# Part border at row tile 42, and the seven row tiles behind it routed as four and three and lined up together

## The reference

```python
xn = _layernorm(x, axis=-1)
x = x + _L0_gnn_ref(xn, src, dst, edge_weight, gnn_weight) + _L0_mix_ref(xn[None], Wqkv, Wout, bout)[0]
x = x + _L0_ffn_ref(_layernorm(x, axis=-1)[None], gate_w, gate_b, w1, b1, w2, b2, gamma, beta)[0]

# _L0_gnn_ref: msgs = x[src] * edge_weight; agg = segment_sum(msgs, dst); agg @ weight      (106250 edges)
# _L0_mix_ref: linear attention, 8 heads of 64; k and v normed per head; out = q (k^T v) / n; Wout, bout
# _L0_ffn_ref: 16 experts, each row goes to its 2 best, weighted by the softmax of the two gate values
h = relu(x @ w1[e] + b1[e])            # 256 -> 512
expert_out = h @ w2[e] + b2[e]         # 512 -> 256
y = x + sum_k topk_w[k] * expert_out[topk_idx[k]]
layernorm(y) * gamma + beta
```

## Time and profile before

| | us |
|---|---|
| median of three runs (1539.89 to 1551.32) | 1547.52 |
| the profiled execution | 1542.19 |
| its span | 1540.5 |
| PE busy | 1077.3 (70%) |
| POOL busy | 1004.7 (65%) |
| DVE busy | 636.2 (41%) |
| ACT busy | 430.5 (28%) |
| mean granted clock of TensorE | 0.867 |

### The profile page before, as it was taken

The page is one execution under the profiler, slowest core; times in us unless marked ns, Lnnn a source line. Parts: engine busy times, 40 slices in busy tenths (PEclk is TensorE's granted clock), DMA queues, the critical chain, the costliest instruction groups (busy, mean ns, idle before and its releaser), DMA issues. The chain is left out here.

```text
span 1540.5 us, 23825 instructions
## 1 busy us (share of the span) xinstructions
PE 1077.3 (70%) x6790; PEld 819.6 (53%) x6790; DVE 636.2 (41%) x2282; ACT 430.5 (28%) x1141; POOL 1004.7 (65%) x1094
## 2 busy tenths in 40 slices
PE   0199989988665979634389659645998975477860
PEld 0055545545543868522278548424876764467750
DVE  7445545543455412324113512250225224554568
ACT  4144434432222333201133223112333322233320
POOL 3477777777647657777767776777776770753425
PEclk9999999999776989965699869866999998599985
DMA  9576566533324888533589479436857770699974
GB/s 337 163 234 221 179 221 194 168 106 104 99 60 149 282 304 299 194 103 105 173 281 343 143 237 344 143 106 228 295 175 220 257 269 14 236 389 317 320 243 136
DMA packets 154922, 323.13 MB, mean 210 GB/s; under 512 B 24768, under 2 KB 97472, under 8 KB 154656
## 3 DMA queue, kind: packets, MB, share of 16 engines
q0 software_dynamic: 49296, 134.68, 27.8%
q1 hardware_dynamic: 65632, 148.16, 27.5%
q10 hardware_dynamic: 39856, 38.67, 7.6%
HBM read 257.06 MB, written 64.36 MB: 209 GB/s over the span
## 5 line engine op out<-in xcount | busy, mean ns | idle before, releaser
L825 POOL DMA_INDIRECT ring<-normed_rows,src_sb x831 | 797.3, 959 | 345.8 <-issue 287.9
L1583 PE MATMUL ps<-room 128*128 128x128 f32 x1888 | 253.5, 292 | 24.6 <-DMA room<-in_w1b 24.2
L1583 PEld LDWEIGHTS ps<-room 128*128 128x128 f32 x1888 | 242.6, 208 | 29.3 <-issue 21.5
L1596 PE MATMUL ps<-room 128*128 128x256 f32 x944 | 227.7, 385 | 11.1 <-issue 10.5
L1451 PE MATMUL ps<-ring,S 128*32 128x256 f32 x1680 | 129.3, 450 | 139.7 <-DMA ring<-normed_rows,src_sb 114.8
L1384 DVE TENSOR_TENSOR desk<-ps,room 128x256 f32<-128x256 f32 x121 | 51.2, 424 | 393.6 <-PE ps L1596 387.3
L1596 PEld LDWEIGHTS ps<-room 128*128 128x128 f32 x944 | 173.2, 194 | 33.4 <-issue 14.2
L1478 PE MATMUL ps<-room,tT 128*128 128x512 f32 x392 | 180.2, 603 | 0.0
L937 ACT ACTIVATE room<-ps,room 128x128 f32<-128x128 f32 x472 | 134.5, 368 | 162.2 <-PE ps L1583 160.5
L816 POOL DMA_INDIRECT ring<-results_by_slot,slot_i x98 | 95.8, 977 | 107.1 <-issue 44.6
L1451 PEld LDWEIGHTS ps<-ring,S 128*32 128x32 f32 x1680 | 57.5, 124 | 188.2 <-issue 158.4
(11 more groups left out here) (206 smaller groups left out, 1255.3 us busy)
## 6 DMA issues: line engine op xcount, KB each, us to landing
room<-in_w2b SPq DMA_DIRECT2D x92, 640.0 KB
room<-in_w1b SPq DMA_DIRECT2D x92, 514.0 KB, 6.4
room<-rows_by_slot SPq DMA_DIRECT2D x121, 128.0 KB
results_by_slot<-desk ACTq DMA_DIRECT2D x121, 128.0 KB
rows_by_slot<-desk ACTq DMA_DIRECT2D x6, 2432.0 KB
ring<-normed_rows,src_sb POOLq DMA_INDIRECT x831
normed_rows<-X SPq DMA_DIRECT2D x7, 896.0 KB, 8.2
result<-ring SPq DMA_DIRECT2D x49, 128.0 KB, 4.6
```

Of the source, the lines that this page charges most:

```text
L825: pool.indirect_dma_start(out=ring[:, b % 2 * BT + m, :], out_offset=None, in_=table, in_offset=bass.IndirectOffsetOnAxis(ap=src_sb[:, b * ...
L1583: mm = pe.matmul(hps[g % 2][:, f * TS:(f + 1) * TS], w1_sb[g % WB][:, k * F + f * P:k * F + (f + 1) * P], xgT[g % 2][:, k, :], start=(k == ...
L1596: mm = pe.matmul(ops, hT[g % 2][:, f, :], w2_sb[g % WB][:, f * D:(f + 1) * D], start=(f == 0), stop=(f == FC - 1))
```

## The change

Four things. The border of the parts moves from row tile 36 to 42, and the subs are cut anew: 24 to 31, 32 to 37, 38 to 41 behind the third, then 42 to 45 and 46 to 48 (before 24 to 29, 30 to 35, 36 to 41, 42 to 46, 47 and 48). The second last sub is JOINED: it gets slots and a scatter but no visits of its own; its full tiles are held, and lined up with those of the last sub, expert by expert, in one run of 25. JOINED was empty before, so the code for it in `line_up`, `runs` and SP's `moe` stood unused. ON_TIME: in slots 68 and 69 the plan adds a visit only if it fits ahead of the landing of the next batch. And a mix that is left for the tail is put first in it.

```diff
-PT = (0, 36, NT)
-SUB = (0, 8, 16, 24, 30, 36, 42, 47, NT)
+PT = (0, 42, NT)
+SUB = (0, 8, 16, 24, 32, 38, 42, 46, NT)
...
-JOINED = ()
+JOINED = (NSUB - 2,)
...
+ON_TIME = 2
+
...
     def chain(work, b):
 
+        if b == NB and mixes:
+
+            g = mixes.pop(0)
+            cost = MIX_PE * (GROUPS[g][1] - GROUPS[g][0])
+            gates.append((g, now + cost + BEHIND[1]))
+            work.append(("mix", g))
+            return cost
...
-        while now < landing(b, b + 1) + LAG:
+        while now < landing(b, b + 1) + (LAG if b < NB - ON_TIME else 0.0):
...
             now += chain(work, b)
-            now += expert(work, b)
+            if b < NB - ON_TIME or now + TAKEN_PE < landing(b, b + 1):
+                now += expert(work, b)
```

## The result

| | before | changed |
|---|---|---|
| median of the runs beside each other | 1547.87 (four) | 1564.47 (four, 1563.02 to 1565.84) |
| ratio, 95% interval | 1 | 1.0109, 1.0077 to 1.0141 |
| the profiled execution, its span | 1542.19, 1540.5 | 1564.56, 1562.8 |
| visits, fresh loads | 118, 92 | 119, 92 |
| T, the end of the last visit | 1492.3 | 1499.8 |

T is here, as in the prediction, the end of PE's last second layer. The changed kernel is slower by 1.1%. Measured once more in another set of runs it had 1569.92 against 1546.84, ratio 1.016 (1.0125 to 1.0195). Both ratios are above 1.01; the interval of the first reaches down to 1.0077. All lines of the changed kernel stand ten higher than before (L1583 is L1593, L1402 is L1412, L825 is L835, L816 is L826).

A forecast was written before the change was run, and what follows sets the result against it. No one engine bounds it all; the end is T plus DVE's finishing work behind it. +4 at T and +15.5 behind it took span 1540.5 to 1560, median said 1565; forecast 1555 to 1577 (chance 0.50), whole range 1537 to 1585.

The forecast's parts named there:

- Total work: Whole kernel: routing rules applied give 119 visits and 92 fresh loads, against 118 and 92 before.
- Start: PE's last long supply of visits, when run 4 begins: at 1127.8 instead of 1060.6, with 63 visits left.
- Slots 60 to 69: PE's stretch before the tail, never without a visit: slot by slot 181.3 us, so the tail begins at 1309.
- rival C: Slower still: POOL's stall comes through, or DVE's slots and line hold tail visits, 10 to 15 more: 1578; chance 0.15.
- The tail of run 5: Slot 70: nine real visits, mix, gates, rank and 8.5 of hold by DVE, 58 us; PE done at 1367.
- The passage: From the end of the tail of run 5 through the left-out run to the joined run's first visit: 14 us, at 1381.
- The joined run: Last run of 25 visits, 16 fresh: 15 x 5.0 + 9 x 3.8 = 109 us, last L1583 at 1490.
- T: End of the last visit: 1490 + 6.3 = 1496.5, that is +4 against the kernel before.
- Behind T: DVE's finishing groups after the last visit: 13 x 4.38 + 2.8, 63.7 us to the end against 48.2, +15.5.
- Sum: Whole kernel: 1540.5 + 4 + 15.5 = 1560 of span; on the median 1567, given as 1565.
- A: Weights no longer late: joined run at 3.8 a step, 91 us, T 18 earlier, 1549; chance 0.22.
- B: Faster: PE packs closer, gates and passages covered, 43 us less, T 1454, 1524; decided by T under 1462; chance 0.13.

The follow-up runs named there:

- Run 4: No follow-up: a run of visits inside the kernel, whose start gives PE its last long supply; first visit at 1060.6 before, 1129.5 in the changed kernel.
- run 8: No follow-up: a run of visits inside the kernel before, 100.6 us for 21 steps, 17 of them into a fresh visit and 4 not.
- packed groups: Both halves of a finishing group between two visits: on the changed kernel 1558.29, ratio 1.0078 (slower chip 2040.66, 1.0063); on the kernel before 2050.05, ratio 1.0094, slower chip.

## Why the prediction was right, point by point

**Total work.** 119 visits and 92 loads, as worked out from the routing rules; L1593 has x1904, 16 to a visit.

**Start.** Said 1127.8, was 1129.5. Run 4's late start is real, and the kernel with an earlier one shows that PE then runs dry instead.

**Slots 60 to 69.** Said 181.3, were 178.0 (1129.47 to 1307.49). The single terms missed by more than their sum: slot 60 took 23.7 for 28, slot 61 17.1 for 19, slot 62 16.4 for 13.5, slot 63 41.0 for 38. The others were within 2. Batch 69 was at 1293.50, said 1294.5. The stop of POOL was 18.9, said 15; batch 66's last gather was issued by 1245 and PE came to it at 1254.5, so it stayed hidden, and that part of rival C is out.

**The tail of run 5.** Said 58 to 1367, was 65 to 1372.9: the worst term, 7 us. The held layer is the row at 1355.33 above. DVE's row of the result before it shows that I named the right cause for it, since it stands directly behind the last operation of the slots:

```profile
1354.67 0.16 DVE L1289 TENSOR_TENSOR prob<-prob 128x3 f32<-128x3 f32 x1
1354.81 0.42 DVE L1394 TENSOR_TENSOR desk<-ps,room 128x256 f32<-128x256 f32 x1
```

But its size was wrong: PE stood idle there for 3.12 us, and I had put 8.5. So all the rest of the tail, which I had at 49.5, took 62.3, and the error in the sum looks smaller than it is. PE waited 3.70 and 2.39 us for ACT and 1.86 for the rank, and ran the tail at a granted clock of 0.84, against 0.94 ahead of it; a first layer took 3.75 us at 1361.07 and 1.95 at 1366.68, which are the two levels, 1.2 and 2.4 GHz. I had priced these visits at 3.9, from a stretch in which the clock stayed up. That the tail came out 7 us dearer is the piece of rival C that came true, but not for C's reason, the hold by DVE, which was smaller than I had put it.

**The passage.** Said 14, was 14.3 (1372.9 to 1387.22).

**The joined run.** Said 109, was 106.4, and 102.8 in the other set. The size was right, the reason only in part. PE's own pace makes 90 of it. Of the 17 us above that, 8.6 are waits for w1 and 2.6 for rows; the first two first layers ran at the lower level of the clock (3.62 and 3.60 us, for 1.95). I took the mean step of run 8, where 21 steps took 22 us above PE's pace and the waits for w1 sum to 13.3, and carried it over to all 15 fresh steps, of which only five waited for w1. With the finishing work largely taken out 98.7 us remain.

**T.** Said 1496.5, was 1499.8. That this is within 3.3 is in part luck: slots 60 to 69 came out 3.3 shorter and the joined run 2.6 shorter than said, start and tail 1.7 and 7 longer.

**Behind T.** Said 63.7, was 63.0: this term carries the verdict. That of the kernel before I explained by DVE's groups "held up a little by picks". The runs with the old border show that the 26 picks give the same 48 us with seven groups, and DVE's waits for picks in the kernel before sum to 2.8 us. The step gave the right number for the changed kernel, where 14 picks need 33 us by estimate and DVE 60. One count in it was short: I had 30 picks left for POOL, and 36 came behind T, the last at 1547.2. That still left DVE's row of the last group, at 1557.8, free of a wait; with packed groups it would be the next limit to look at.

**Sum.** Said 1560 of span, was 1562.8 and 1562.7; 1565 on the median, was 1564.5 and 1569.9. On the spans of the two kernels +7.5 at T and +14.8 behind it make +22.3; the forecast had +4 and +15.5. On the medians it is +16.6 and +23.1.

**The rivals.** A (weights no longer late, T 18 earlier) fell: even with DVE's groups, the stores and most of the picks taken out, T is only 5 us earlier. My argument against it was weaker than it looked. I held 400 GB/s against the best stretch, 331, but the page of the kernel before has a slice of 38.5 us at 389:

```profile
GB/s 337 163 234 221 179 221 194 168 106 104 99 60 149 282 304 299 194 103 105 173 281 343 143 237 344 143 106 228 295 175 220 257 269 14 236 389 317 320 243 136
```

In the window 1348.0 to 1386.4 of that kernel the DMA engines are at a share of 1.02, so 389 is the most that they are seen to move when full, and A's 400 lies above it. What kept A from coming true are the 17 us above PE's pace, told under the joined run. Weights were still late where the DMA engines were near full, and not where they weren't. Two windows of the changed kernel; the first has no wait for w1, the second has two, 2.09 and 1.56 us:

```profile
1440.00:1460.00 20.00, 19.11 (x132) 17.60 (x132) 12.58 (x38) 8.22 (x28) 11.35 (x12) 1.00 0.78 243
1460.00:1480.00 20.00, 15.72 (x104) 13.92 (x104) 10.31 (x32) 6.42 (x22) 7.59 (x8) 1.00 0.96 312
```

A mean over the run, 302 GB/s, hides this. The Trainium skill, "DMA: Bandwidth & Descriptors", section Bandwidth, on which A leaned, puts a ceiling of 435 GB/s beside one of about 358 for what a core moves from and to HBM; the slice of 389 lies between the two: it is above the second, and no run here reaches the first. B (T under 1462) fell by 38 us: gates waited as before, and the passage was paid in full. C is true in part, as told: the tail was 7 us dearer, with a hold by DVE of 3 us in it; POOL's stop did not come through.

## What to carry to other kernels

A border behind which results may be used only all together sets two things at once: how late the finishing work can begin, and how much of it must come last. Before moving one to fill a hole ahead of it, count the finishing groups that will stand behind the last visit and price them at the full time of their engine; here that term of 15 us was paid, and the 25 us by which the hole was shortened gave nothing, since the supply ahead of it had been made later by 69. And ask whether the end is set by the engine that is busy in the rows or by a stream that feeds it: in the kernel before the picks alone come to 48 us and DVE's groups, without their waits for picks, to some 45, and packing the groups gained nothing.

## What the runs showed of the hardware

Three of the chips ran all kernels that were tried on them a third slower, the kernel before at 2019 to 2092 us. Most instructions take as long there as elsewhere (in the kernel without the join and in the changed one, mean of one: gathers 957 and 961 ns, the relu 369 and 368, the bias 425 and 425; the second layer, at a lower mean clock, 429 and 385). But PE shows idle gaps of 0.3 to 1.1 us in the middle of a group of matmuls, put down to issue; of the kernel without the join, on a slower chip:

```profile
419.67 0.38 PE L1461 MATMUL ps<-ring,S 128*32 128x256 f32 x1 [0.84 <-issue]
420.39 0.32 PE L1478 MATMUL ps<-ident,X 128*128 128x128 f32 x1 [0.34 <-issue]
421.80 0.37 PE L1478 MATMUL ps<-ident,X 128*128 128x128 f32 x1 [1.09 <-issue]
423.20 6.02 PE L1488 MATMUL ps<-room,tT 128*128 128x512 f32 x8 [1.03 <-issue]
```

Groups of the same line are whole elsewhere (x24 in 1.50 us). The mean granted clock was 0.78 to 0.80, against 0.84 to 0.87, and POOL waited 416 to 496 us in all for PE's edges, against 58 in the kernel before and 66 in the changed one. That PE gets its instructions late on these chips is what the gaps look like; the cause was not looked for and stays open. An experiment on a rate that PE sets can't be read on such a chip. What lies behind T can be read only with care. With packed groups it was as long as on the ordinary chip (38.7 and 38.6 us). But in four runs with 13 or 14 groups behind T it took 70.4 to 75.1 us, where 14 took 63 on the ordinary one: for a stretch of a few groups DVE has gaps of its own there, such as this one in the kernel without the join:

```profile
2015.71 0.88 DVE L1442 SCALAR_TENSOR_TENSOR ring<-ring,f_r,aggT 128x256 f32<-128x256 f32 x2 [3.23 <-remote]
```
